# A transformer block in fp32 pairs on one core: three of four batches of x read already transposed, and three seams rearranged

## The reference

```python
x = x + layernorm(attention(layernorm(x), w_qkv, b_qkv, w_o, b_o))
x = x + layernorm(ffn(layernorm(x), gate_w, base_w, base_b, lora_A, lora_B))
# layernorm: (x - mean) / sqrt(var + 1e-5) over the last axis, no weights
# attention: 32 query heads, 8 key/value heads of 32, rotary embedding, causal softmax
# ffn: x @ base_w.T + base_b + 2 * sum over 8 experts of (x @ A_e.T) @ B_e.T,
#      weighted by a softmax over the two largest of 8 gate logits
```

## Time and profile before

| | before |
|---|---|
| median of 3 runs | 1020.37 us |
| the profiled execution: its time | 1019.11 us |
| its span, first to last instruction | 1017.4 us |
| TensorE busy | 993.5 us (98%) |
| VectorE busy | 662.9 us (65%) |
| GpSimd busy | 450.7 us (44%) |
| ScalarE busy | 400.4 us (39%) |
| mean granted TensorE clock | 0.997 |
| TensorE on the chain that ended last | 93% |
| HBM read, written | 85.20 MB, 40.37 MB |

### The profile page before, as it was taken

The page is one execution under the profiler, slowest core; times in us unless marked ns, Lnnn a source line. Parts: engine busy times, 40 slices in busy tenths (PEclk is TensorE's granted clock), DMA queues, the critical chain, the costliest instruction groups (busy, mean ns, idle before and its releaser), DMA issues.

```text
span 1017.4 us, 17424 instructions
## 1 busy us (share of the span) xinstructions
PE 993.5 (98%) x6408; PEld 816.2 (80%) x6408; DVE 662.9 (65%) x1954; ACT 400.4 (39%) x682; POOL 450.7 (44%) x489
## 2 busy tenths in 40 slices
PE   6999999999999999999999999999999999999996
PEld 5889888898885666666666669999999999999996
DVE  6753443334557889988999867666666666666654
ACT  6431321210126877777777662222222222222211
POOL 1443542432437999999998820111111111111110
PEclk9999999999999999999999999999999999999999
DMA  9342342228237786755555373222222222222101
GB/s 355 128 166 83 125 145 103 84 104 207 83 143 194 183 216 185 188 158 146 148 141 153 117 233 105 86 83 83 83 83 83 83 83 82 83 79 76 55 22 41
DMA packets 78644, 127.23 MB, mean 125 GB/s; under 512 B 7776, under 2 KB 46944, under 8 KB 75488
## 3 DMA queue, kind: packets, MB, share of 16 engines
q1 hardware_dynamic: 78560, 126.13, 41.0%
HBM read 85.20 MB, written 40.37 MB: 123 GB/s over the span
## 4 chain that ended last, share of the span: by engine, by line
PE 93%; DMA 3%; ACT 1%; DVE 1%; POOL 1%; SPq 0%; issue 0%; POOLq 0%
PE bank L1312 21%; PE bank L1314 21%; PE bank L1313 21%; PE bank L1384 8%; PE bank L1422 7%; PE bank L1406 7%; PE bank L1321 2%; DMA q_t<-shift_l 1%; PE bank L1443 1%; PE bank L1583 1%; PE bank L1449 1%; DMA wf_raw<-w_ffn 1%; PE bank L1452 1%; ACT prob L850 0%; PE bank L1478 0%
## 5 line engine op out<-in xcount | busy, mean ns | idle before, releaser
L1033 DVE CUSTOM_DVE_ANT_0 bank<-bank,row_mask 128x384 f32<-128x384 f32 (+3 forms) x512 | 236.1, 519 | 53.4 <-PE bank L1384 53.2
L662 POOL TENSOR_TENSOR ln_rs<-ln_ve,minus_half 128x1 f32<-128x1 f32 x64 | 59.8, 934 | 395.9 <-DVE ln_mm L977 395.9
L850 ACT ACTIVATE prob<-bank 128x512 f32<-128x512 f32 x320 | 173.6, 599 | 35.2 <-PE bank L1406 29.0
L1312 PE MATMUL bank<-wf_h,xt_h 128*128 128x384 f32 (+1 forms) x384 | 129.7, 338 | 0.9 <-DVE z L1197 0.9
L1314 PE MATMUL bank<-wf_l,xt_h 128*128 128x384 f32 (+1 forms) x384 | 130.1, 339 | 0.0
L1313 PE MATMUL bank<-wf_h,xt_l 128*128 128x384 f32 (+1 forms) x384 | 129.6, 338 | 0.0
L1384 PE MATMUL bank<-k_t,q_t 96*128 96x384 f32 (+3 forms) x512 | 123.1, 337 | 0.0
L1312 PE MATMUL bank<-xt_h,wq_h 128*128 128x512 f32 x304 | 119.8, 394 | 0.0
L1314 PE MATMUL bank<-xt_l,wq_h 128*128 128x512 f32 x304 | 118.6, 390 | 0.0
L1313 PE MATMUL bank<-xt_h,wq_l 128*128 128x512 f32 x304 | 118.5, 390 | 0.0
L720 POOL TENSOR_TENSOR key_sum<-key_sum,prob 128x512 f32<-128x512 f32 x92 | 116.6, 1292 | 0.0
(11 more groups left out here) (118 smaller groups left out, 1904.3 us busy)
## 6 DMA issues: line engine op xcount, KB each, us to landing
q_t<-q_scratch SPq DMA_DIRECT2D x32, 512.0 KB, 5.3
q_scratch<-turn_h SPq DMA_DIRECT2D x16, 512.0 KB, 2.7
q_scratch<-turn SPq DMA_DIRECT2D x16, 512.0 KB, 2.9
q_t<-q_scratch SPq DMA_DIRECT2D x32, 256.0 KB, 5.6
att_scratch<-att SPq DMA_DIRECT2D x32, 256.0 KB, 2.5
at_raw<-att_scratch SPq DMA_DIRECT2D x16, 512.0 KB, 3.8
x<-x SPq DMA_DIRECT2D x16, 512.0 KB, 4.2
out<-z SPq DMA_DIRECT2D x15, 512.0 KB, 2.9
```

The source lines that it names most:

```text
L662: nc.gpsimd.tensor_tensor(ln_rs[j][:], ln_ve[j][:], minus_half[:], ALU.pow).then_inc(count, 1)
L850: nc.scalar.activation(prob[n % 2][:, i, :, :].rearrange("p h q -> p (h q)"), score_bank(n, i)[:], ACT.Exp, scale=INV_SQRT_HD).then_inc(pr ...
L1033: last = nc.vector.tensor_tensor_reduce(out=row, in0=row, in1=row_mask[:, SEQ - w:SEQ], scale=1.0, scalar=LOWEST, op0=ALU.add, op1=ALU.max ...
L1312: mm(dst, a_h, w_h, start=start, stop=False, skip_group_check=True)
```

## The change

- **Batches 1 to 3 of x** are also passed transposed (`x_t`). The kernel loads them into the place of `xt_l` (`load_turned`, four DMAs of 512 KB a batch). The rows of x are still loaded for the statistics. Power and minus mean of four tiles are packed into `ln_pack`, turned by one transpose a batch (`transpose_pack`), copied, stored to HBM and loaded back broadcast over all partitions (`store_stats`, `load_stats`, 512 KB written to SBUF). VectorE adds the minus mean and multiplies by the root in two passes over each quarter (`normalise_turned`), ScalarE makes the high part (`turned_to_hi`), VectorE the low part (`turned_to_lo`). The 12 tile transposes, their copies and their low parts are gone, and so is the normalisation on ScalarE. The first pair of a batch waits for its quarters one at a time.
- **Attention**: T stands ahead of V2 instead of behind R2, with its cast ahead of the value copy on ScalarE and its low part one unit earlier on VectorE. The shift of group 1 is loaded ahead of the last two stores of v. In the group before the last two, T stands ahead of D, and the first out-projection no longer waits for the last shift.
- **Tile 0 of stage 3**: `normalise_x1(0)` stands ahead of `split_ffn(4)` on ScalarE, `transposed2(0)` ahead of `copy_sums`.
- **Last tile**: blocks of 392, 512 and 256 columns, chunks in plain order so that the first four need only one half of `lo2`; the sum of the tile before in the order half, block 0, half, rest; three chunks of block 2 ahead of the first LoRA products; statistics in three parts; one half of the last residual on VectorE straight from the root, the other on ScalarE and VectorE.

```diff
 LOWEST = -3.0e38
 OUT_SPLIT = (KC + 1) * D
 FFN_COLS = [(0, AGW + 256), (AGW + 256, 384), (AGW + 640, 384)]
+LAST_COLS = [(0, AGW + 256), (AGW + 256, 512), (AGW + 768, 256)]
+LAST_STATS = [(0, 512), (512, 256), (768, 256)]
...
-XRING = 3
+XRING = 2
+TURNS = 4
+TURN = KC // TURNS
...
-ORDER = ("S0 R0 R1 S1 S2 V0 V1 V2 V3 R2 T R3 R4 "
+ORDER = ("S0 R0 R1 S1 S2 V0 V1 T V2 V3 R2 R3 R4 "
          "S3 S4 S5 R5 D S6 R6 R7 S7 R8 S8 S9 R9 R10").split()
-ORDER_OUT = [("S0 S1 S2 V0 V1 V2 V3 S3 S4 S5 D T S6 S7 O0 S8 O1 S9 O2 "
+ORDER_OUT = [("S0 S1 S2 V0 V1 V2 V3 S3 S4 S5 T D S6 S7 O0 S8 O1 S9 O2 "
...
+            def load_turned(b, g):
+                wait(sp, proj_ps, 2 * USES * (b - 1) if b >= 2 else 0)
+                chunks = slice(TURN * g, TURN * g + TURN)
+                sp.dma_start(xt_raw[b % 2][:, chunks, :], x_t[b - 1, :, chunks, :]
+                             ).then_inc(turned_loaded[g], 16)
+
+            def store_stats(b):
+                sp.wait_ge(pack_copied, b)
+                sp.dma_start(stat_scratch[b - 1].rearrange("s (t p) -> (s t) p", p=P), pack_t[:]
+                             ).then_inc(stats_stored, 16)
+
+            def load_stats(b):
+                sp.wait_ge(stats_stored, 16 * b)
+                wait(sp, turned_norm, TURNS * (b - 1))
+                sp.dma_start(token_stats[:], stat_scratch[b - 1].partition_broadcast(P)).then_inc(stats_loaded, 16)
 
...
+                        store_stats(after)
+                        load_stats(after)
+                    if t < NT and p == 2:
+                        load_x(t)
+                        load_x(t + 1)
                     if b == BATCH - 1 and p == 3:
                         load_shift(0)
                 for t in range(TT * b, TT * b + TT):
+                    if t == NT - 2:
+                        load_shift(1)
...
+                    load_x(TT * (b + 2) + 3)
 
...
 
             for n in range(NG):
-                if n + 1 < NG:
...
             def store_out(t):
-                for i, cols in enumerate(final_cols(t)):
-                    sp.wait_ge(z_step, 9 * t + 9 + i)
-                    sp.dma_start(out[t][:, cols], z[:, cols]).then_inc(out_stored, 16)
+                sp.wait_ge(z_step, 9 * t + 9)
+                sp.dma_start(out[t], z[:]).then_inc(out_stored, 16)
+
+            def store_last(t):
+                sp.wait_ge(z_step, 9 * t + 11)
+                sp.dma_start(out[t][:, HALF:D], z[:, HALF:D]).then_inc(out_stored, 16)
+                sp.wait_ge(z_norm, t + 2)
+                sp.dma_start(out[t][:, 0:HALF], z[:, 0:HALF]).then_inc(out_stored, 16)
 
             for t in range(NT + 1):
                 if 0 < t < NT - 2:
...
+                nc.gpsimd.tensor_tensor(ln_pack[t // TT - 1][:, 1, t % TT:t % TT + 1], ln_ve[t % LN][:],
+                                        minus_half[:], ALU.pow).then_inc(ln1_norm, 1)
+
+            root(TT)
...
-                    if t is not None and t + 2 < NT:
-                        scale1(t + 2)
+                    if b + 1 < BATCH and p == 0:
+                        root(TT * (b + 1) + 2)
+                        root(TT * (b + 1) + 3)
+                if b + 2 < BATCH:
+                    root(TT * (b + 2))
+                    root(TT * (b + 2) + 1)
 
...
+            def copy_pack(b):
+                act.wait_ge(pack_ps, b)
+                wait(act, stats_stored, 16 * (b - 1))
+                nc.scalar.copy(pack_t[:], bank[0][0:2 * TT, 0:P]).then_inc(pack_copied, 1)
+
+            def turned_to_hi(b, g):
+                if g == 0:
+                    act.wait_ge(xt_ps, TT)
+                    wait(act, proj_ps, 2 * USES * (b - 1))
+                act.wait_ge(turned_norm, TURNS * (b - 1) + g + 1)
+                chunks = slice(TURN * g, TURN * g + TURN)
+                nc.scalar.copy(xt_h[b % 2][:, chunks, :], xt_raw[b % 2][:, chunks, :]
+                               ).then_inc(turned_hi, 1)
 
...
-                    shift_to_hi(n + 1)
                 exps(n, 3)
                 exps(n, 4)
                 if 1 <= n <= NPIECE:
                     piece_hi(n - 1)
...
                     copy_sums(n - 1)
-                    if n == NG - 2:
-                        shift_to_hi(n + 1)
...
 
             def normalise_z(t):
                 act.wait_ge(z_scale, 2 * t + 2)
-                for cols in final_cols(t):
-                    nc.scalar.activation(z[:, cols], z[:, cols], ACT.Identity, bias=ln_nm[1][:],
-                                         scale=ln_rs[1][:]).then_inc(z_norm, 1)
+                nc.scalar.activation(z[:], z[:], ACT.Identity, bias=ln_nm[1][:], scale=ln_rs[1][:]).then_inc(z_norm, 1)
+
+            def normalise_last(t):
+                act.wait_ge(z_scale, 2 * t + 2)
+                nc.scalar.activation(z[:, HALF:D], z[:, HALF:D], ACT.Identity, bias=ln_nm[1][:], scale=ln_rs[1][:]
+                                     ).then_inc(z_norm, 1)
+                act.wait_ge(z_step, 9 * t + 10)
+                nc.scalar.activation(z[:, 0:HALF], z[:, 0:HALF], ACT.Identity, bias=ln_nm[1][:]).then_inc(z_norm, 1)
 
             split_att(1)
             split_ffn(2)
...
             def stats1(t):
                 x_wait(dve, t)
-                wait(dve, xn_ready, t - LN + 1)
-                statistics(x_in(t), t % LN, ln1_step, 5 * t)
+                minus_mean = None
+                if t < TT:
+                    wait(dve, xn_ready, t - LN + 1)
+                elif t < TT + LN:
+                    dve.wait_ge(xn_ready, t - LN + 1)
+                else:
+                    dve.wait_ge(ln1_norm, 2 * TT + t - LN - TT + 1)
+                if t >= TT:
+                    minus_mean = ln_pack[t // TT - 1][:, 0, t % TT:t % TT + 1]
+                statistics(x_in(t), t % LN, ln1_step, 5 * t, minus_mean)
...
+            def normalise_turned(b, g):
+
+                if g == 0:
+                    dve.wait_ge(stats_loaded, 16 * b)
+                dve.wait_ge(turned_loaded[g], 16 * b)
+                part = xt_raw[b % 2][:, TURN * g:TURN * g + TURN, :]
+                minus_mean, root = [token_stats[:, s, :].unsqueeze(1).broadcast_to([P, TURN, SEQ]) for s in range(2)]
+                nc.vector.tensor_tensor(part, part, minus_mean, ALU.add).then_inc(turned_centred, 1)
+                dve.wait_ge(turned_centred, TURNS * (b - 1) + g + 1)
+                nc.vector.tensor_tensor(part, part, root, ALU.mult).then_inc(turned_norm, 1)
+
+            def turned_to_lo(b, g):
+
+                dve.wait_ge(turned_hi, TURNS * (b - 1) + g + 1)
+                chunks = slice(TURN * g, TURN * g + TURN)
+                nc.vector.tensor_tensor(xt_l[b % 2][:, chunks, :], xt_raw[b % 2][:, chunks, :],
+                                        xt_h[b % 2][:, chunks, :].bitcast(F32), ALU.subtract
+                                        ).then_inc(turned_ready, 1)
...
             for b in range(BATCH - 1):
+                t = TT * (b + 1)
                 for p in range(PAIRS):
                     rope_half(b, p, 0)
                     rope_half(b, p, 1)
-                    t = tile_after(b, p)
-                    if t is not None:
-                        next_tile(t)
-                for t in range(TT * b, TT * b + TT):
-                    v_bias(t)
+                    if p == 0:
+                        stats1(t + 2)
+                        stats1(t + 3)
+                    elif p == 2:
+                        normalise_turned(b + 1, 0)
+                        normalise_turned(b + 1, 1)
+                    elif p == 3:
+                        turned_to_lo(b + 1, 0)
+                        turned_to_lo(b + 1, 1)
+                        normalise_turned(b + 1, 2)
+                    elif p == 4:
+                        turned_to_lo(b + 1, 2)
+                        normalise_turned(b + 1, 3)
+                v_bias(TT * b)
+                v_bias(TT * b + 1)
+                turned_to_lo(b + 1, 3)
+                v_bias(TT * b + 2)
+                v_bias(TT * b + 3)
+                if t + TT < NT:
+                    stats1(t + TT)
+                    stats1(t + TT + 1)
             b = BATCH - 1
-            dve.wait_ge(xt_ps, NT)
+            dve.wait_ge(turned_norm, TURNS * (BATCH - 1))
             dve.wait_ge(proj_ps, 2 * USES * (BATCH - 1))
             for slot in range(SLOTS):
                 nc.vector.memset(k_t[slot][KROWS:P, :].bitcast(F32), 1.0).then_inc(k_ones, 1)
...
                             if kind == "R":
                                 maxima(n, j)
-                            if (kind, n, j) == ("R", 1, 3):
+                            if (kind, n, j) == ("R", 1, 2):
...
+                ffn_add(t, 0)
+                ffn_add(t, 1)
+                dve.wait_ge(z_step, s + 2)
+                last_part(0)
+                last_part(1)
+                ffn_add(t, 2)
+                dve.wait_ge(z_step, s + 5)
+                last_part(2)
+                moments(1, z_step, s + 4, parts=ln_last[:])
...
```

(115 more changed lines are left out.)

140 lines of the change are left out of this document (64 added, 76 removed).

## The result

The changed kernel takes 1009.01 us (median of 4 runs, 1007.73 to 1010.47), the kernel before 1019.7 in the same series. The ratio is 0.9894, interval 0.9876 to 0.9912: 1.1% faster and clear of noise, by 10.7 us, where 19.4 were forecast. 1009.0 lies above the range (998.5 to 1007). The profiled execution took 1007.73 us, its span is 1005.7.

A forecast was written before the change was run, and what follows sets the result against it. TensorE was taken as the bound, busy 993.5 of 1017.4 us. Terms -10.0 - 3.6 - 2.2 - 0.9 - 2.1 = -18.8 from 1019.11 gave 1000.3, with half of 1.26 added 1001.0 us; range 998.5 to 1007.

The forecast's parts named there:

- Transposes, -10.0: Projection: removing 12 tile transposes of 0.87 us saves 10.4 us, three small added ones cost 0.4; net -10.0 us.
- Transposes were a cover: Rival, chance 0.04: TensorE arrives 0.87 us sooner at banks VectorE, ScalarE or SyncE must free; half the 10 stays, 1006 us.
- What replaces them, 0: Projection: normalising turned x on VectorE and ScalarE is ready in time for TensorE, so it costs 0 us.
- as TensorE ends v: 0: Later projection batches: even with passes of 2.29 us, VectorE's work ends as TensorE ends v, costing 0 us.
- this rival: Batch 0 of projection is late through broadcast on full queues or blocked passes: +6 to +8, 1007 to 1009 us; chance 0.15.
- First seam, -3.6: Start of attention's second group: an earlier shift load removes TensorE's 2.30 us stall and the slow clock behind it; -3.6 us.
- The share of the clock, 1.3: Second attention group: V units after the stall took 3.63 us instead of 2.36; without the stall 1.3 us is saved.
- Groups, -2.2: Attention groups: earlier T sends the shift's DMA out about 1 us earlier, removing stalls; -2.2 us, range 0 to -2.7.
- Group 30 and tile 0, -0.9: Before and at the start of stage 3: a 0.7 us shift wait and 0.3 us ahead of the transposes go; -0.9 us.
- last tile, -2.1: End of stage 3: shorter waits for z and low_l, smaller last block, residual halves on two engines; -2.1 us.
- the 0.63 that was put on: Whole kernel: half of the 1.26 us by which the median of runs exceeds the profiled execution, added to the forecast.
- The landing of the statistics: Projection, batch 0: store issued at about 52.5, some 3 us to store, 4.5 to broadcast; landed at 60.5 us.

The follow-up runs named there:

- experiment 3: Changed kernel with the mask and the loads of group 0 issued ahead of the last two V stores of batch 2: 1003.78 us, ratio 0.9851.
- experiment 6: Changed kernel with GpSimd's rope operations in pairs 3 and 4 of batch 2 cut from 512 to 64 columns, for timing alone: 1004.78 us, ratio 0.9844.
- experiment 8: The repaired kernel with the second shift's load moved back behind the loads of V and of the first output weights: 1002.12 us, ratio 0.9823.
- experiments 1 and 2: Changed kernel with T back behind R2 and the former copy and maxima order: 1007.08 us; changed kernel with T between V3 and R2: 1000.77 us.
- experiment 7: Kernel before the change with only T moved to between V3 and R2, and the copy and maxima orders this needs: 1014.3 us, ratio 0.994.
- the repaired kernel: Changed kernel with T right behind V3 and the loads of group 0 issued earlier: 996.56 us and, in another series, 995.66 us.
- experiment 5: The repaired kernel with T moved from behind V3 to ahead of V0: 1027.41 us, ratio 1.0071.

## Why the prediction was wrong

*Transposes, -10.0:* right, -10.4 by experiment 3. "Transposes were a cover" has to be split. For the banks of the rotations, by which it was priced, it was false. But it also named things that SyncE must free sooner, and the load of keys was one: 4.2 of the 10.4 us were lost there.

*What replaces them, 0: this step failed,* in the sentence on the later batches, "as TensorE ends v: 0". It asked only whether TensorE waits for VectorE, and it lengthened only VectorE's passes. GpSimd's operations beside them grow as well, and SP waits for these: in its queue stand the store of keys, V's four stores, the mask and the loads of group 0, in this order. SP's queue in the changed kernel:

```profile
213.02 5.78 SPq L488 DMA_DIRECT2D v_scratch<-v_out  x4
218.84 0.43 SPq L557 DMA_DIRECT2D row_mask<-row_mask  x1
219.38 0.53 SPq L507 DMA_DIRECT2D q_t<-q_scratch  x1
...
221.04 0.55 SPq L510 DMA_DIRECT2D k_t<-k_scratch  x1
```

and the same steps on the chain that ended last, as it comes through them:

```profile
212.62 0.36 SPq L484
...
213.53 4.40 DMA v_scratch<-v_out
218.03 0.44 DVE v_out L1103
...
221.04 5.61 DMA k_t<-k_scratch
226.70 0.66 PE bank L1542 x4
```

The V sum on it, the last of four, is late by this chain and not by the passes: VectorE stood for V's buffer, which was still being stored.

```profile
218.03 0.42 DVE L1103 TENSOR_TENSOR v_out<-bank,bias_v 128x256 f32<-128x256 f32 x1 [1.56 <-DMA v_scratch<-v_out]
```

The kernel before had room for almost nothing there. GpSimd's last operations, the store of keys and the load of keys before:

```profile
218.82 2.55 POOL L682 TENSOR_TENSOR turn<-turn,turn_h 128x512 f32<-128x512 f32 x2
221.40 0.36 SPq L455 DMA_DIRECT2D k_scratch<-turn  x1
...
230.04 0.55 SPq L480 DMA_DIRECT2D k_t<-k_scratch  x1
```

The load landed at 235.9, and the first row score started at 236.35: 0.5 us of margin that no wait shows. The change took 10.4 us from TensorE's way to this score. By the same mark, the first product of 512 columns, GpSimd begins this rotation 9.9 us earlier (216.32 and 204.59). Its four operations then take 8.0 us instead of 5.05, so it ends only 7.0 earlier, and the loads gained 7.2 (230.04 - 28.99 against 221.04 - 27.19). 10.4 - 7.2 - 0.5 = 2.7, for a measured stop of 2.57. The clock adds 1.7. So of the lateness 2.9 us come from GpSimd's longer operations and 0.5 from VectorE's passes ahead of the rotation (experiment 6 has these 0.5 back: GpSimd begins at 205.43, 176.9 behind its mark, against 177.4).

The rule that the prediction weighed is borne out. The Trainium skill (page "SBUF — State Buffer", section "Who interferes with whom") calls the port pair that VectorE and GpSimd share an exclusive lock, and says that a VectorE instruction with two SBUF inputs contends with a GpSimd instruction that reads SBUF. The trace agrees, for both engines. The 12 centring passes have a median of 2.31 us, 1.22 where GpSimd is idle; in experiment 6 a GpSimd operation of 64 columns takes 0.32 us alone and 1.23 beside a pass, which runs from 205.93 to 207.15:

```profile
205.43 0.32 POOL L727 TENSOR_TENSOR turn<-turn 128x64 f32<-128x64 f32 x1 [6.20 <-DVE turn L1095]
206.09 1.23 POOL L730 TENSOR_TENSOR turn<-turn 128x64 f32<-128x64 f32 x1 [0.34 <-DVE turn L1095]
```

But it was weighed at the wrong place. The prediction put its harm in batch 0, at the banks of the rotations, and on VectorE alone. There TensorE never waited: the statistics had landed by 56.7 us (predicted 60.5), and three of the first four passes, from 58 to 62 us, ran at 1.22 to 1.23 with GpSimd idle. The harm came in batch 2, where 0 was booked. That the time of 1009 is also the upper end of this rival is chance.

*First seam, -3.6:* right, -3.9 between the marks, and 3.8 when it is undone (experiment 8). The share of the clock, 1.3, is borne out too: slow V units come back with the stop, 1.15 us longer.

*Groups, -2.2: this step failed.* "T moves ahead of V2, V3 and R2" counted what T lets start earlier, and nothing for T's place on TensorE itself. The gain was there, though less than predicted: waits fell from 2.6 to 1.2 us over 26 groups. The price was 0.16 us in each of them, 4.2 us, shown in one order by experiments 1 and 2 and in the kernel before by experiment 7. The row of the table spans 29 groups: 29 x 0.16 is 4.6, less the 1.4 of waits 3.2, for +3.4 measured. Before, T takes 273 ns, and after it 277; what changes is the distance between its neighbours, and for that the prediction had no term.

*Group 30 and tile 0, -0.9, and last tile, -2.1:* together -3.0 between the marks, as predicted (-1.0 of it ahead of V of group 31: 596.74 and 587.34). The waits of the earlier trace rows for z and low_l fell to 0.2 each. They were not tested apart, so this agreement is of the sum alone.

*The range.* The bounds of the terms add up to -20.2 and -13.1, that is 999.5 to 1006.6 us with the 0.63 that was put on; "999 to 1003.5 from the bounds of the terms" was narrower than they are. The landing of the statistics, 52.5 + 3 + 4.5, is 60.0 and not 60.5. Neither slip made the failure.

With both failed steps repaired the kernel takes 995.7 to 996.6 us, 4 to 5 below the forecast of 1001.0: the repaired T also takes back the 4.2 us that its old place had cost.

Open: why T costs 0.16 us more among row scores and 0.32 more among V's tiles. The loads of weights ahead of T show idle time of 0.6 us each in the changed kernel, but no run parts this from the shape of the tiles. Open too is what delays the shift in the groups (5 to 8 of 26 in the repaired kernel) that still run over 8.80 us.

## What to carry to other kernels

When an edit makes the bounding engine arrive earlier, look for each thing that it meets next and take its margin from the trace, loads included: landing time against first use. A wait of zero in the profile may be a margin of 0.5 us. For work that moves to another engine, follow the queues behind it to their end, and those behind the work that it runs beside (here GpSimd's rotation, the store of keys, V's stores, the loads), not only to its first reader. A small matmul has no price of its own: put it where the engine changes from one kind of work to another, and measure the distance between its neighbours, not its duration.

## What the runs showed of the hardware

- The same transpose of 128 columns lengthens TensorE's work by 0.01, 0.17 or 0.33 us by its place (3.96, 4.12 and 4.28 against 3.95 us without it): behind tiles of 32 columns and ahead of row scores, among row scores, among tiles of 32 columns. Ahead of such tiles, and behind a stop, 0.21 us pass between its start and theirs (experiment 5).
- VectorE passes with two SBUF inputs take 1.22 us alone and 2.2 to 2.3 beside GpSimd's operations; these go from 1.27 to 2.25 us (two in 2.54 alone, two in 4.50 beside them). Both engines pay, in batches 0 to 2 of the changed kernel.
- A stop of TensorE of 2.6 us was followed by some 3.5 us at half the clock, which cost 1.7 us more at batch 3 (0.43 instead of 0.23 us a matmul). At the first seam, after a stop of 2.6 us as well, the V units alone took 1.15 us more (experiment 8).
- The start of the program differs between executions: the first product of 512 columns starts at 27.2 to 27.3 us in three profiles and at 28.4 to 29.0 in the other nine.
